# Four turns of the probabilities, moved between the products of a head of queries

## The chip, the cores and the metric

The kernel runs on one core of a Trainium2 chip. The metric is the device time of one execution in microseconds. TensorE (PE) multiplies, VectorE (DVE), ScalarE (ACT) and GpSimd (POOL) do the elementwise work, SyncE (SP) issues most of the transfers. All engines run their own instructions in order and wait for each other on semaphores.

## What is computed

A residual block with four parts over x of 8 sequences x 128 tokens x 512. The change lies in the second, an attention with adapters: 32 query heads in 8 groups of 4, one key and value head for each group, head size 128.

```python
x = x + L0(x)                       # a linear layer chosen by sequence
q = rope(x @ wq + (x @ aq[id]) @ bq[id])      # 32 heads of 128
k = rope(x @ wk + (x @ ak[id]) @ bk[id])      # 8 heads
v = x @ wv + (x @ av[id]) @ bv[id]            # 8 heads
p = softmax(where(causal & mask, q k^T / sqrt(128), min))
o = p v
x = x + o @ wo + (o @ ao[id]) @ bo[id]
x = x + L2(x);  x = x + L3(x)       # two more adapter layers
```

All is float32. Wide products are done in three passes over a high and a low part of both operands (hi x hi, hi x lo, lo x hi), so most operands have an `_hi` tile made on ScalarE and an `_lo` tile made by VectorE or GpSimd.

## The kernel before

A first stage computes L0, keys, values and the first queries. The last computes L2 and L3. Between them stands the loop over heads: `over_heads` (L826) runs `slots(g, first, last)` for the 8 groups g of heads, the first and the last written out, the six between as a loop on each engine. A group has eight slots b = 0 to 7, one for each sequence; slot t = 8g + b treats tile t, the 4 heads of the group for sequence b.

In slot t TensorE does, in this order:

1. `scores` of tile t (L1109): 4 heads, each in two products of 128 columns, into `ps_s`. In the slots b = 0 and b = 4 they need the rotated queries of the next half of sequences, which means all four heads up to the slot just before (`q_done`).
2. `turn` of tile t - 1 (L1118): four transposes of 128 x 128, one a head, of the probabilities into one bank `ps_t`. It waits for `prob_done` and `pt_lo_done`, and the fourth turn signals `t_ready`.
3. `queries` of one head (`project`, L74 to L85): for each of four parts k of the width the products L78, L79, L80 with 512 columns, then two adapter products L83; signals `q_ready`. A head is projected for four sequences at once, so four slots fill one half. The slots t = 60 to 63 have no queries.
4. `outputs` of tile t - 2 (L1140 to L1150), which waits for `ot_lo_done` and for `res_done`.
5. `values` of tile t - 1 (L1126 to L1128), which waits for `pt_lo_done`.

ScalarE in slot t: `pt` (L913, the copy `pt_hi` of `ps_t`, waits for `t_ready`), then the four exponentials of tile t (L929, wait for `max_done`), then parts of weights (wq_hi L896, bq L900; in b = 1 also the four wo_hi L903 and, at the end, ao_hi), and `ot_hi` (L919) of tile t - 1.

VectorE in slot t: maximum and scaling (L1049, `sm`), `ot_lo` of t - 2 (L1026), the additions to `res` and `axo` of t - 3 (L1031, L1032), `pt_lo` of t - 1 (L1022), the reciprocal of tile t (L1064, waits for the exponentials), `rotate` (L1006 `qc`, L1008 twice `qs`, waits for `q_ready`), in odd b `bq_lo` (L1013), in b = 1 `wo_lo` (L1018).

GpSimd in slot t: the probabilities times the reciprocal (L980, `prob_done`), the sum of the rotation `qt` (L973, waits for `qs`, signals `q_done`), wq_lo (L965) in b < 4, and in b = 1 three wo_lo (L989) and ao_lo (L992).

SyncE loads the next group's weights, keys and values. None of its waits names a signal of the turns.

Of the kernel before, what the change touches and what calls it, by code (L numbers as in the profile page):

```python
# [30 lines left out]
def program(nc, x, xt, lora_ids, pos, attn_ids, slot_ids, mask, w0, wq, wk, wv, wo, a3, bq, bk, bv, ao, bo,  # L31
# [9 lines left out]
    B, T, HID = x.shape  # L41
    KC = HID // P
    D = P
    KVH, _, _, GW = wq.shape
    G = GW // D
    R = a3.shape[4]
    NT = B * T
    assert R == R_PACK and KC * R * 2 == P
    HALF = B // 2
    HT = HALF * T  # L50
    PAIRS = B // 2
# [12 lines left out]
    with whole:  # L64
        def sb(ctx, name, shape, dt=F32):
            return ctx.enter_context(nc.sbuf_tensor(name, shape, dt))
# [4 lines left out]
        def sem(ctx, name):  # L71
            return ctx.enter_context(nc.semaphore(name))

        def project(pe, bank, w_hi, w_lo, b_pack, ax, cols, half):  # L74

            tok = slice(half * HT, (half + 1) * HT)
            for k in range(KC):
                pe.matmul(bank[:, :], w_hi[:, k, cols], x1t_hi[:, k, tok], start=(k == 0), stop=False)  # L78
                pe.matmul(bank[:, :], w_hi[:, k, cols], x1t_lo[:, k, tok], start=False, stop=False)  # L79
                pe.matmul(bank[:, :], w_lo[:, k, cols], x1t_hi[:, k, tok], start=False, stop=False)  # L80
            for pair in range(PAIRS // 2):
                n = half * PAIRS // 2 + pair
                last = pe.matmul(bank[:, pair * 2 * T:(pair + 1) * 2 * T], b_pack[:, n, cols],  # L83
                                 ax[:, n * 2 * T:(n + 1) * 2 * T], start=False, stop=(pair == PAIRS // 2 - 1))
            return last  # L85

        res = sb(whole, "res", [P, B, HID])
        ident = sb(whole, "ident", [P, P])
# [26 lines left out]
        axt = [axt_all[:, n, :] for n in range(2)]  # L115
# [56 lines left out]
        ps_t, ps_ao, ps_out, ps_o, ps_q = ps_x1, ps_ax, ps_p[0], ps_p[1], ps_p[2:4]  # L172
# [608 lines left out]
        with ExitStack() as c:  # L781

            wq_raw, bq_raw, wq_hi, wq_lo, bq_pack = raw_w, raw_b, wgt_hi[0], wgt_lo[0], packs[0]
# [10 lines left out]
            prob = [sb(c, f"prob{i}", [P, G, T]) for i in range(2)]  # L794
# [14 lines left out]
            q_ready = sem(c, "q_ready")  # L809
# [5 lines left out]
            prob_done = sem(c, "prob_done")  # L815
            t_ready = sem(c, "t_ready")
            pt_hi_done = sem(c, "pt_hi_done")
            pt_lo_done = sem(c, "pt_lo_done")
# [7 lines left out]
            def over_heads(eng, slots):  # L826

                slots(0, True, False)
                with eng.Fori(1, KVH - 1) as g:
                    slots(g, False, False)  # L830
                slots(KVH - 1, False, True)

            with nc.Block() as block:
# [249 lines left out]
                @block.tensor  # L1083
                def _(pe):
                    project_tensor(pe)

                    def queries(n, half, h, weights=None):

                        if not isinstance(n, int) or n >= 2:
                            pe.wait_ge(q_mult, 3 * (n - 1))  # L1090
                        else:
                            pe.wait_ge(k_mult, 3 * (VU + G - 1 + n))
                        if weights:
                            pe.wait_ge(wq_lo_done, weights[0])
                            pe.wait_ge(bq_lo_done, weights[1])
                        project(pe, ps_q[h % 2], wq_hi, wq_lo, bq_pack, axt[0], slice(h * D, (h + 1) * D), half).then_inc(q_ready, 1)

                    def scores(t, g, b):
                        half = b // HALF
                        if isinstance(t, int) and t == 0:  # L1100
                            pe.wait_ge(k_done, VU + G)
                        if not isinstance(g, int) or g + half >= 1:
                            pe.wait_ge(q_done, B * g + G * half)
                        pe.wait_ge(kt_in[half], 16 * (g + 1))
                        if not isinstance(t, int) or t >= 2:
                            pe.wait_ge(max_done, t - 1)
                        at = (b % HALF) * T
                        for h in range(G):
                            mm = pe.matmul(ps_s[b % 2][:, h, :], qt[:, half, h, at:at + T], kt[:, b * T:(b + 1) * T], start=True, stop=True)  # L1109
                        mm.then_inc(s_ready, 1)  # L1110

                    def turn(t, b):
                        t_parity = b % 2
                        pe.wait_ge(prob_done, t + 1)
                        if not isinstance(t, int) or t >= 1:
                            pe.wait_ge(pt_lo_done, t)
                        for h in range(G):
                            mm = pe.transpose(ps_t[:, h * T:(h + 1) * T], prob[t_parity][:, h, :], ident[:, :])  # L1118
                        mm.then_inc(t_ready, 1)

                    def values(t, g, b):
                        pe.wait_ge(v_in[b // HALF], 32 * (g + 1))
                        pe.wait_ge(pt_lo_done, t + 1)
                        if not isinstance(t, int) or t >= 1:
                            pe.wait_ge(ot_lo_done, t)
                        pe.matmul(ps_o[:, :], v_hi3[:, b, :], pt_hi[:, :], start=True, stop=False)  # L1126
                        pe.matmul(ps_o[:, :], v_hi3[:, b, :], pt_lo[:, :], start=False, stop=False)
                        pe.matmul(ps_o[:, :], v_lo3[:, b, :], pt_hi[:, :], start=False, stop=True).then_inc(o_ready, 1)  # L1128

                    def outputs(t, g, b):  # L1130
                        pe.wait_ge(ot_lo_done, t + 1)
                        if not isinstance(t, int) or t >= 1:
                            pe.wait_ge(res_done, t)
                        for h in range(G):
                            q = slice(h * T, (h + 1) * T)
                            if b == 0 and h == 0:
                                pe.wait_ge(wo_lo_done, g + 1)
                            elif b == 0:
                                pe.wait_ge(wo_lo_pool, (G - 1) * g + h)
                            pe.matmul(ps_out[:, :], ot_hi[:, q], wo_hi[:, h, :], start=(h == 0), stop=False)  # L1140
                            pe.matmul(ps_out[:, :], ot_hi[:, q], wo_lo[:, h, :], start=False, stop=False)  # L1141
                            pe.matmul(ps_out[:, :], ot_lo[:, q], wo_hi[:, h, :], start=False, stop=(h == G - 1))  # L1142
                        if b == 0:
                            pe.wait_ge(ao_lo_done, g + 1)
                        pe.wait_ge(axo_done, t + 1)
                        for h in range(G):
                            q = slice(h * T, (h + 1) * T)
                            w = ao_pack[:, b, h, :, :].rearrange("p a r -> p (a r)")
                            pe.matmul(ps_ao[0:2 * R, 0:T], w, ot_hi[:, q], start=(h == 0), stop=False)
                            mm = pe.matmul(ps_ao[0:2 * R, 0:T], w, ot_lo[:, q], start=False, stop=(h == G - 1))  # L1150
                        mm.then_inc(out_ready, 1)

                    def slots(g, first, last):
                        for b in range(B):
                            t = B * g + b
                            scores(t, g, b)
                            if not first or b >= 1:
                                turn(t - 1, (b - 1) % B)
                            if b < HALF:
                                queries(t, 1, b, None if first else (G * g, PAIRS * g))  # L1160
                            elif not last:
                                queries(t, 0, b - HALF, (G * g + b - HALF + 1, PAIRS * g + 2))
                            if not first or b >= 2:
                                outputs(t - 2, g - 1 if b < 2 else g, (b - 2) % B)
                            if not first or b >= 1:
                                values(t - 1, g - 1 if b < 1 else g, (b - 1) % B)

                    over_heads(pe, slots)
                    end, g = B * KVH, KVH - 1
                    turn(end - 1, B - 1)  # L1170
                    outputs(end - 2, g, B - 2)
                    values(end - 1, g, B - 1)
                    outputs(end - 1, g, B - 1)
# [389 lines left out]
```

## Time and profile before

| | us |
|---|---|
| median of 3 runs | 825.22 |
| lowest and highest | 823.1, 829.45 |
| profiled execution | 820.86 |
| its span, first to last instruction | 819.2 |
| TensorE busy | 752.1 |
| VectorE busy | 543.8 |
| GpSimd busy | 325.6 |
| ScalarE busy | 324.1 |

The span is that of the profiled execution; the time includes what lies around it. Matmuls are pipelined, so that the durations of neighbouring rows overlap: how long a product holds TensorE is read from the starts of successive rows. A weight load (PEld) has a row of its own.

### The profile page before, as it was taken

What the parts mean: (1) busy time and instruction counts of PE and PEld (TensorE: products, weight loads), DVE (VectorE), ACT (ScalarE), POOL (GpSimd) and SP (SyncE); (2) the same over time, 40 slices, a digit from 0 to 9 for tenths busy, and PEclk for the clock granted to TensorE, in tenths of its full rate; (3) what the DMA queues carried; (4) which work ended last, traced back from release to release, by engine and by line L of the source; (5) the groups of instructions that cost most, each with busy time, mean ns of one, the idle gap of its engine ahead of it and who ended that gap; (6) DMA issues with size and microseconds to landing.
All of it is one profiled execution on the core that took longest, in us unless ns stands there. A gap on an engine that the chain in (4) does not pass through costs nothing. (4 is left out here: it accounts for less than half of the span.)

```text
span 819.2 us, 13219 instructions
## 1 busy us (share of the span) xinstructions
PE 752.1 (92%) x4100; PEld 625.0 (76%) x4100; DVE 543.8 (66%) x1362; ACT 324.1 (40%) x902; POOL 325.6 (40%) x280
## 2 busy tenths in 40 slices
PE   2888897985889999999999999999999999998798
PEld 2777785764668888888888888888888888876586
DVE  3645577676576767767677667758676875654983
ACT  3555343011153454354345435336343533542540
POOL 2334351453374273346237236335523723510320
PEclk8798997997899999999999999999999999999899
DMA  8776787264313024013212303301311110720502
GB/s 265 232 282 201 223 259 226 96 220 167 128 65 117 1 74 164 9 64 118 61 45 83 115 0 121 123 0 64 132 47 55 73 38 3 161 20 7 128 25 78
DMA packets 61498, 87.87 MB, mean 107 GB/s; under 512 B 18118, under 2 KB 35686, under 8 KB 57878
## 3 DMA queue, kind: packets, MB, share of 16 engines
q1 hardware_dynamic: 41714, 73.53, 27.8%
q10 hardware_dynamic: 17188, 8.46, 3.5%
q0 software_dynamic: 2560, 5.45, 2.2%
q8 instruction: 17, 0.28, 0.1%
q14 instruction: 19, 0.16, 0.1%
HBM read 72.45 MB, written 19.68 MB: 112 GB/s over the span
## 5 line engine op out<-in xcount | busy, mean ns | idle before, releaser
L980 POOL TENSOR_TENSOR prob<-prob,rinv 128x512 f32<-128x512 f32 x64 | 66.6, 1041 | 215.6 <-DVE rinv L1064 215.6
L919 ACT ACTIVATE ot_hi<-ps_p_o 128x512 fp32r<-128x512 f32 x64 | 38.0, 594 | 214.7 <-PE ps_p_o L1128 214.7
L78 PE MATMUL ps_p_q<-x1t_hi,wgt_hi 128*128 128x512 f32 x280 | 115.9, 414 | 0.8 <-DVE qt L618 0.8
L973 POOL TENSOR_TENSOR qt<-qc,qs 128x512 f32<-128x512 f32 x60 | 83.7, 1395 | 77.8 <-DVE qs L1008 77.8
L929 ACT ACTIVATE prob<-sm,nmax 128x128 f32<-128x128 f32 x256 | 99.8, 392 | 31.2 <-DVE nmax L1049 30.1
L80 PE MATMUL ps_p_q<-x1t_hi,wgt_lo 128*128 128x512 f32 x280 | 110.9, 396 | 0.0
L79 PE MATMUL ps_p_q<-x1t_lo,wgt_hi 128*128 128x512 f32 x280 | 110.8, 396 | 0.0
L1140 PE MATMUL ps_p_out<-wo_hi,ot_hi 128*128 128x512 f32 x256 | 101.9, 398 | 6.6 <-DVE ot_lo L1026 4.7
L1141 PE MATMUL ps_p_out<-wo_lo,ot_hi 128*128 128x512 f32 x256 | 101.4, 396 | 0.0
L1142 PE MATMUL ps_p_out<-wo_hi,ot_lo 128*128 128x512 f32 x256 | 100.8, 394 | 0.0
L1008 DVE TENSOR_TENSOR qs<-ps_p_q,trig 64x512 f32<-64x512 f32 x120 | 82.6, 688 | 3.7
L1049 DVE CUSTOM_DVE_ANT_0 sm<-ps_y_s,maskbias 128x128 f32<-128x128 f32 x256 | 59.0, 286 | 31.4 <-issue 31.0
L1109 PEld LDWEIGHTS ps_y_s<-kt,qt 128*128 128x128 f32 x512 | 67.1, 193 | 12.4 <-POOL qt L682 3.8
L1109 PE MATMUL ps_y_s<-kt,qt 128*128 128x128 f32 x512 | 69.0, 278 | 4.9 <-POOL qt L682 3.6
L80 PEld LDWEIGHTS ps_p_q<-x1t_hi,wgt_lo 128*128 128x128 f32 x280 | 52.8, 189 | 12.4
L1140 PEld LDWEIGHTS ps_p_out<-wo_hi,ot_hi 128*128 128x128 f32 x256 | 48.3, 189 | 17.5 <-DVE ot_lo L1026 6.5
L78 PEld LDWEIGHTS ps_p_q<-x1t_hi,wgt_hi 128*128 128x128 f32 x280 | 53.3, 190 | 10.3 <-DVE qt L618 1.0
L79 PEld LDWEIGHTS ps_p_q<-x1t_lo,wgt_hi 128*128 128x128 f32 x280 | 53.0, 189 | 9.4
L1046 DVE MEMSET gate<- 128x1 f32 x64 | 3.8, 59 | 81.8 <-PE ps_y_s L1109 81.8
L1142 PEld LDWEIGHTS ps_p_out<-wo_hi,ot_lo 128*128 128x128 f32 x256 | 48.0, 187 | 11.5
L1006 DVE TENSOR_TENSOR qc<-ps_p_q,trig 128x512 f32<-128x512 f32 x60 | 41.4, 689 | 21.0 <-PE ps_p_q L83 21.0
L913 ACT ACTIVATE pt_hi<-ps_x_t 128x512 fp32r<-128x512 f32 x64 | 38.1, 596 | 42.8 <-PE ps_x_t L1118 42.6
(227 smaller groups left out, 1693.8 us busy)
## 6 DMA issues: line engine op xcount, KB each, us to landing
raw_w<-in_wq SPq DMA_DIRECT2D x8, 1024.0 KB, 4.9
raw_b<-bq_sel SPq DMA_DIRECT2D x64, 128.0 KB
wo_raw<-in_wo SPq DMA_DIRECT2D x8, 1024.0 KB, 4.9
qt<-in_w SPq DMA_DIRECT2D x5, 1024.0 KB, 9.1
v_hi_d<-v_hi ACTq DMA_DIRECT2D x16, 256.0 KB, 3.7
v_lo_d<-v_lo ACTq DMA_DIRECT2D x16, 256.0 KB, 5.3
kt<-k_rot SPq DMA_DIRECT2D x16, 256.0 KB, 3.7
v_hi<-v_hi_d SPq DMA_DIRECT2D x16, 256.0 KB, 3.9
```

What stands on the lines that cost most here:

```text
L78: pe.matmul(bank[:, :], w_hi[:, k, cols], x1t_hi[:, k, tok], start=(k == 0), stop=False)
L79: pe.matmul(bank[:, :], w_hi[:, k, cols], x1t_lo[:, k, tok], start=False, stop=False)
L80: pe.matmul(bank[:, :], w_lo[:, k, cols], x1t_hi[:, k, tok], start=False, stop=False)
L929: e = act.activation(prob[i][:, h, :], sm[:, h, :], ACT.Exp, bias=nmax[i][:, h:h + 1], scale=-1.0, accum_out=rsum[i][:, h:h + 1])
L973: pool.tensor_tensor(qt[:, half, h, :], qc[:, :], qs[:, :], ALU.add).then_inc(q_done, 1)
L980: pool.tensor_tensor(prob[i][:, :, :], prob[i][:, :, :], rinv[i][:, :].unsqueeze(2).broadcast_to([P, G, T]), ALU.mult).then_inc(prob_done, 1)
L1008: dve.tensor_tensor(qs[to:to + 64, :], ps_q[i][at:at + 64, :], sin_t[to:to + 64, tok], ALU.mult).then_inc(q_mult, 1)
L1049: m = dve.tensor_tensor_reduce(out=sm[:, h, :], in0=ps_s[i][:, h, :], in1=maskbias[:, b, :], scale=-1.0, scalar=3.0e38, op0=ALU.add, op1=A ...
L1109: mm = pe.matmul(ps_s[b % 2][:, h, :], qt[:, half, h, at:at + T], kt[:, b * T:(b + 1) * T], start=True, stop=True)
L1140: pe.matmul(ps_out[:, :], ot_hi[:, q], wo_hi[:, h, :], start=(h == 0), stop=False)
L1141: pe.matmul(ps_out[:, :], ot_hi[:, q], wo_lo[:, h, :], start=False, stop=False)
L1142: pe.matmul(ps_out[:, :], ot_lo[:, q], wo_hi[:, h, :], start=False, stop=(h == G - 1))
```

## The change

`project` gets an argument `between`, a function that it calls behind the first product (L78) of each part k. The turns are cut into `turn_head`, one head each: head 0 does the two waits, head 3 signals. In `slots`, where a slot has queries and a tile to turn, the turns are handed to `queries` as `between`; the slots of the last group with b >= 4 keep `turn` at its old place, as does the end.

```diff
-        def project(pe, bank, w_hi, w_lo, b_pack, ax, cols, half):
+        def project(pe, bank, w_hi, w_lo, b_pack, ax, cols, half, between=None):
             tok = slice(half * HT, (half + 1) * HT)
             for k in range(KC):
                 pe.matmul(bank[:, :], w_hi[:, k, cols], x1t_hi[:, k, tok], start=(k == 0), stop=False)
+                if between:
+                    between(k)
                 pe.matmul(bank[:, :], w_hi[:, k, cols], x1t_lo[:, k, tok], start=False, stop=False)
                 pe.matmul(bank[:, :], w_lo[:, k, cols], x1t_hi[:, k, tok], start=False, stop=False)
...
-                    def queries(n, half, h, weights=None):
+                    def queries(n, half, h, weights=None, between=None):
...
+                    def turn_head(t, b, h):
+                        if h == 0:
+                            pe.wait_ge(prob_done, t + 1)
+                            if not isinstance(t, int) or t >= 1:
+                                pe.wait_ge(pt_lo_done, t)
+                        mm = pe.transpose(ps_t[:, h * T:(h + 1) * T], prob[b % 2][:, h, :], ident[:, :])
+                        if h == G - 1:
+                            mm.then_inc(t_ready, 1)
+
                     def turn(t, b):
-                        t_parity = b % 2
-                        pe.wait_ge(prob_done, t + 1)
-                        if not isinstance(t, int) or t >= 1:
-                            pe.wait_ge(pt_lo_done, t)
                         for h in range(G):
-                            mm = pe.transpose(ps_t[:, h * T:(h + 1) * T], prob[t_parity][:, h, :], ident[:, :])
-                        mm.then_inc(t_ready, 1)
+                            turn_head(t, b, h)
...
                             scores(t, g, b)
-                            if not first or b >= 1:
+
+                            turned = (lambda h, t=t, b=b: turn_head(t - 1, (b - 1) % B, h)) if not first or b >= 1 else None
+                            if b < HALF:
+                                queries(t, 1, b, None if first else (G * g, PAIRS * g), turned)
+                            elif not last:
+                                queries(t, 0, b - HALF, (G * g + b - HALF + 1, PAIRS * g + 2), turned)
+                            else:
                                 turn(t - 1, (b - 1) % B)
-                            if b < HALF:
-                                queries(t, 1, b, None if first else (G * g, PAIRS * g))
-                            elif not last:
-                                queries(t, 0, b - HALF, (G * g + b - HALF + 1, PAIRS * g + 2))
```

## Rows read from the trace of the kernel before

**Rows 1.** The page, busy time, share and instructions of each engine

```profile
PE 752.1 (92%) x4100; PEld 625.0 (76%) x4100; DVE 543.8 (66%) x1362; ACT 324.1 (40%) x902; POOL 325.6 (40%) x280
```

**Rows 2.** TensorE's timeline, slot b = 3: start, us, engine, line, operation, tiles, count

```profile
441.04 1.05 PE L1109 MATMUL ps_y_s<-kt,qt 128*128 128x128 f32 x8
441.93 0.60 PE L1118 MATMUL ps_x_t<-ident,prob 128*128 128x128 f32 x4
442.28 0.48 PE L78 MATMUL ps_p_q<-x1t_hi,wgt_hi 128*128 128x512 f32 x1
442.60 0.40 PE L79 MATMUL ps_p_q<-x1t_lo,wgt_hi 128*128 128x512 f32 x1
...
445.17 0.39 PE L83 MATMUL ps_p_q<-axt_all,pack 128*128 128x256 f32 x2
445.40 0.40 PE L1140 MATMUL ps_p_out<-wo_hi,ot_hi 128*128 128x512 f32 x1
...
449.41 1.05 PE L1109 MATMUL ps_y_s<-kt,qt 128*128 128x128 f32 x8
...
500.31 1.05 PE L1109 MATMUL ps_y_s<-kt,qt 128*128 128x128 f32 x8
```

**Rows 3.** Timeline of the weight loads in the same slot

```profile
442.25 0.19 PEld L78 LDWEIGHTS ps_p_q<-x1t_hi,wgt_hi 128*128 128x128 f32 x1
442.37 0.19 PEld L79 LDWEIGHTS ps_p_q<-x1t_lo,wgt_hi 128*128 128x128 f32 x1
```

**Rows 4.** TensorE's timeline, two adapter products of the same slot

```profile
448.25 0.22 PE L1150 MATMUL ps_ax_ao<-ot_lo,ao_pack 128*32 128x128 f32 x1
448.31 0.22 PE L1149 MATMUL ps_ax_ao<-ot_hi,ao_pack 128*32 128x128 f32 x1
```

**Rows 5.** Timelines of ScalarE and VectorE, slots b = 2 and b = 3

```profile
435.26 0.58 ACT L913 ACTIVATE pt_hi<-ps_x_t 128x512 fp32r<-128x512 f32 x1
435.74 0.40 ACT L929 ACTIVATE prob<-sm,nmax 128x128 f32<-128x128 f32 x1
...
437.19 0.20 ACT L929 ACTIVATION_READ_ACCUMULATOR prob<-sm,nmax 128x1 f32 x1
...
442.56 0.60 ACT L913 ACTIVATE pt_hi<-ps_x_t 128x512 fp32r<-128x512 f32 x1 [0.73 <-PE ps_x_t L1118]
...
437.42 0.18 DVE L1064 RECIPROCAL rinv<-rsum 128x4 f32<-128x4 f32 x1 [0.47 <-ACT prob L929]
437.51 0.68 DVE L1006 TENSOR_TENSOR qc<-ps_p_q,trig 128x512 f32<-128x512 f32 x1
...
445.60 0.69 DVE L1006 TENSOR_TENSOR qc<-ps_p_q,trig 128x512 f32<-128x512 f32 x1 [0.37 <-PE ps_p_q L83]
```

**Rows 6.** GpSimd's timeline, the rotated queries in slots b = 3 and b = 7

```profile
447.82 1.29 POOL L973 TENSOR_TENSOR qt<-qc,qs 128x512 f32<-128x512 f32 x1 [1.46 <-DVE qs L1008]
...
481.34 1.86 POOL L973 TENSOR_TENSOR qt<-qc,qs 128x512 f32<-128x512 f32 x1 [1.46 <-DVE qs L1008]
```

**Rows 7.** TensorE's timeline around a late slot b = 7, and its waits

```profile
474.57 1.05 PE L1109 MATMUL ps_y_s<-kt,qt 128*128 128x128 f32 x8
...
483.43 1.15 PE L1109 MATMUL ps_y_s<-kt,qt 128*128 128x128 f32 x8 [0.31 <-POOL qt L973]
...
PE ps_y_s L1109 <- POOL qt L973: 1.2, 4, 0.3
```

**Rows 8.** VectorE's timeline: a slot's first work, and the end of slots b = 7 and b = 1

```profile
442.23 0.29 DVE L1049 CUSTOM_DVE_ANT_0 sm<-ps_y_s,maskbias 128x128 f32<-128x128 f32 x1
...
443.68 0.68 DVE L1031 TENSOR_TENSOR res<-ps_p_out,res 128x512 f32<-128x512 f32 x1
...
481.30 0.75 DVE L1013 SCALAR_TENSOR_TENSOR pack<-pack,lows,raw_b 128x512 fp32r<-128x512 f32 x1
...
498.64 1.89 DVE L1013 SCALAR_TENSOR_TENSOR pack<-pack,lows,raw_b 128x512 fp32r<-128x512 f32 x1
500.48 1.75 DVE L1018 TENSOR_TENSOR wo_lo<-wo_raw,wo_hi 128x512 fp32r<-128x512 f32 x1
```

More of the change, by code:

```diff
@@ L1095, in queries @@
                             pe.wait_ge(bq_lo_done, weights[1])
-                        project(pe, ps_q[h % 2], wq_hi, wq_lo, bq_pack, axt[0], slice(h * D, (h + 1) * D), half).then_inc(q_ready, 1)
+                        project(pe, ps_q[h % 2], wq_hi, wq_lo, bq_pack, axt[0], slice(h * D, (h + 1) * D), half, between).then_inc(q_ready, 1)
                     def scores(t, g, b):
```

## The prediction

> **What bounds the kernel now.** I read the page first: TensorE is busy 752.1 of 819.2 us [rows 1]. Then TensorE's timeline over one slot of the loop over heads, the slot b = 3 of a middle round [rows 2]. It runs from 441.04 (first product of the scores) to 449.41, so a slot is 8.37 to 8.39 us, and in it TensorE never idles: the scores take 0.89 us until the turns, L78 starts 0.35 us after the first turn, the other products follow each other, and L1140 starts 4.36 us into the slot. Eleven products from L79 (442.60) to L83 (445.17) take 2.57 us, 0.233 us each. There are 64 slots; the turns fall inside queries in 59 of them (t = 1 to 59; t = 0 has no turn, t = 60 to 63 no queries).
>
> A saturated TensorE is half of the answer. The list of waits shows the other half: the scores waited for GpSimd's rotated queries L973 four times [rows 7]. Only the scores of b = 0 and b = 4 wait for a rotation of the slot just before (`q_done`), so the chain that ends in L973 is measured there. I followed it backwards. In the slot b = 3, qt ends at 447.82 + 1.29 = 449.11 and the scores need it at 449.41 less some 0.2. In the slot b = 7 that began at 474.57, qt took 1.86 us, ended at 483.20, and the scores came at 483.43: 8.86 us for that slot in place of 8.39 [rows 6, 7]. So the chain to the next half of the queries has almost no slack, and every delay in it stops TensorE once in four slots: 8 times behind b = 3 and 7 times behind b = 7. By the starts of L1109, five of those seven b = 7 slots are already late, four by 0.47 and one by 0.3 us, 2.2 us in all (one of them stands in [rows 7]).
>
> **The change, TensorE's side.** No instruction is added or removed. The four turns leave the place ahead of L78 and each follows one of the four L78. What does a turn cost in each place? A weight load starts when the product before it starts: L79's load at 442.37 marks the true start of L78, though L78's row begins at 442.28, and L78's load at 442.25 marks the fourth turn [rows 2, 3]. From the first turn (441.93) to 442.37 are 0.44 us for four turns, 0.11 each, and L79 starts 0.23 us after that, the usual spacing. So one turn costs the load that follows it, 0.11 us, because 128 columns stream in less than that. Between L78 and L79 the turn's own load hides under L78, but L79's load starts only with the turn, and L79 can start 0.11 us later. Four turns cost 0.44 us in either place: I take 0 for TensorE's work. The bounds: the pairs L1149 and L1150, 128 columns with a load of only 32, follow each other in 0.06 us [rows 4]. If a turn came down to that, 4 x 0.05 = 0.2 us of a slot would be saved. At the other end a turn that exposed its own load as well would cost 0.22 us, 0.44 us more a slot. I stay at 0.11, because the next load has started with the product before it in every row here.
>
> The Trainium skill, page "TensorE: Matmul & The Clock Gate", section "Back-to-back issue gap", gives a warm gap of about 56 ns for 128 columns, and its section on the array's architecture says that TensorE's queue can pull weight loads ahead of products in flight. By that rule an interleaved turn costs 0.056 us in place of 0.11, an estimate of 0.21 us saved a slot. It is the rule behind the first rival below. The rows of the block of turns, at 0.11 each, side with the same page's section on LDWEIGHTS (128 columns in 107 ns).
>
> **The other side: the last turn comes later.** `t_ready` rises with the fourth turn. It now starts 442.25 - 441.04 = 1.21 us into the slot. With the change L78 truly starts at 0.89, the first turn at 0.89 + 0.233, and the fourth three groups of three products and one turn later: 1.12 + 3 x (0.70 + 0.11) = 3.55 us. That is 2.34 us later. Behind `t_ready` stands ScalarE, in order: pt_hi (L913) first, and only then the four exponentials of the next tile (L929). So the exponentials, though their input is ready, are held until pt_hi. The value products themselves come behind the adapter products of [rows 4], over 7.2 us into the slot, and don't suffer.
>
> How far is it from pt_hi to the rotation? A slot b = 2 shows it, for there pt_hi is late already: pt_hi 435.26, first exponential 435.74, last sum read at 437.39, rinv 437.42, qc 437.51, so 2.25 us from pt_hi to qc [rows 5]. From qc to qt are 447.82 - 445.60 = 2.22 us [rows 5, 6]. pt_hi starts 0.31 us after the fourth turn (442.56 against 442.25). New slot: fourth turn 3.55, pt_hi 3.86, qc 6.11 (now 4.56, held only by the product L83), qt 8.33, end 9.62 us with 1.29 or 10.19 with 1.86, scores 0.23 later: 9.85 or 10.42 in place of 8.38. Nothing hides this, for TensorE works in order and stands at the scores.
>
> **The sum.**
> - Behind b = 3, 8 times, qt at 1.29 us as in these slots now: 8 x 1.47 = 11.8 us.
> - Behind b = 7, 7 times, with qt at 1.86 in five as now: 7 x 1.47 + 5 x 0.57 - 2.2 already there = 10.9 us.
> - After such a stop the eight products of the scores take 1.15 instead of 1.05 us [rows 2, 7]: ten further stops, 1.0 us.
> - The slot b = 2 of rounds 1 to 6. VectorE's bq_lo (L1013) and wo_lo (L1018) stand behind the rotation in b = 1. When they alternate with GpSimd's work they take 1.89 and 1.75 us and end at 502.23, 1.92 us behind the scores of 500.31 (that slot's start). 1.55 us later they end at 3.47; from the first sm to the end of the addition to res are 444.36 - 442.23 = 2.13 us; with some 0.2 for the signal L1140 starts at 5.8 in place of 4.36: 1.45 us of stop [rows 2, 8]. Where bq_lo goes first (0.75 us, qt then 1.86) the same sum ends at some 4.75: 0.4. Three of each: 5.5 us, bounds 2.4 and 8.7.
> - The first round: slot t = 1 has no outputs, so the value products follow the queries 4.36 us into it; pt_hi starts at 3.86 and takes 0.6, pt_lo about as long [rows 5], the signal 0.2: 5.3, so 0.9 us, once.
> - Waits added to TensorE's queue (`prob_done`, `pt_lo_done` behind the first L78): the probabilities are ready long before; 0. No DMA is moved or waits for these signals: 0.
>
> Together 30.1 us. Whether VectorE or GpSimd goes first in each slot moves this: all qt at 1.29 and b = 2 at its low bound give some 24, all at 1.86 with the high bound some 39. The profiled execution took 820.9 us, so it becomes 851.0. The median of the runs shown is 4.4 us above it (825.2), which I carry over: 855.
>
> **The rivals.**
> - *The turns' cost halves on TensorE.* At 0.06 each, 44 slots save 0.2, the 15 slots that end in a stop save only what the fourth turn gains, 3 x 0.05: together 11 us. The late chain remains: 19 us slower, 844. For it: the pairs at 0.06 [rows 4]. Against it: their load is a quarter of a turn's, and the block of turns at 0.11.
> - *Not slower: the hold does not reach TensorE.* If the exponentials were not held by pt_hi, or the queries' rotation had slack of 1.5 us, the late turns would cost nothing: 825 with turns at 0.11, and 813 with turns at 0.06 (59 x 0.2 = 11.8 us less). It is faster by over 1% once a turn costs less than 0.075 us. Against it stand the order on ScalarE and the slots with 8.86 us, where 0.57 us more on qt already stopped TensorE [rows 6, 7].
> - *A turn between products costs more.* At 0.22 us, 44 x 0.44 plus 15 x 0.33 us are 24 more: 879. For it only that no row shows a turn behind a 512-column product; against it L83 to L1140, where the kinds change without a gap.
>
> **How the numbers follow.** The forecast holds 78%, the halved turns 12%, the hold that does not reach 6%, the dearer turns 4%. 24 to 39 us on 820.9, with and without the 4.4 us of the median, is 845 to 864; the first rival brings the lower end to 842, and I stop at 863. About 1% is what a measurement of this kernel can tell from no change. Faster 3%, same 4%, slower 93%.
>
> **What would show it.** Right: the slots inside a half stay at 8.4 us, slots b = 3 and b = 7 show 9.8 to 10.4 with TensorE waiting at L1109 for L973, some 25 us in all; pt_hi starts 3.9 us into a slot, the exponentials directly behind it; L79 follows a turn by 0.11. A stop at L1140 in slots b = 2. Wrong: slots inside a half at 8.2 (turns cheaper) or 8.8 (dearer); exponentials that start before pt_hi; scores of b = 4 on time.

## The result and the profile after

| | before | after |
|---|---|---|
| median | 824.5 us (4 runs) | 853.18 us (4 runs, 849.87 to 858.49) |
| ratio, 95% interval | | 1.0354 (1.0320 to 1.0389) |
| profiled execution | 820.86 us | 858.49 us |
| its loop over heads, first scores to last slot's end | 527.5 us | 559.6 us |

The kernel became 3.5% slower. The profiled execution after is the slowest of the four. It is 37.6 us longer than the profiled execution before. Of these, 32.1 lie in the loop; the unchanged first stage took 4.3 us more (it ends anywhere between 213 and 221 us in the profiles of this study) and the last stage 1.2.

Line numbers moved by the edit: the scores are L1112, the turns L1120, the products L79, L82, L83, the adapter products L86, pt_hi L916, the exponentials L932, qt L976, qc L1009, the outputs L1147. The kernels of the experiments have line numbers of their own.

The list of waits of TensorE after the change (engine, tile, line, who released it: us in total, times, longest) answers [rows 7], where the first line stood at 1.2 us in 4 times:

```profile
PE ps_y_s L1112 <- POOL qt L976: 19.2, 15, 1.8
...
PE ps_p_out L1147 <- DVE ot_lo L1029: 10.6, 8, 2.5
```

Fifteen stops at the scores, exactly the slots behind b = 3 and b = 7, and a second group at the outputs. Here is one slot b = 3 after the change, the same group of heads and slot as in [rows 2], which now begins at 463.44. TensorE's timeline first:

```profile
463.44 1.06 PE L1112 MATMUL ps_y_s<-kt,qt 128*128 128x128 f32 x8
464.25 0.48 PE L79 MATMUL ps_p_q<-x1t_hi,wgt_hi 128*128 128x512 f32 x1
464.57 0.27 PE L1120 MATMUL ps_x_t<-ident,prob 128*128 128x128 f32 x1
464.60 0.48 PE L82 MATMUL ps_p_q<-x1t_lo,wgt_hi 128*128 128x512 f32 x1
464.91 0.39 PE L83 MATMUL ps_p_q<-x1t_hi,wgt_lo 128*128 128x512 f32 x1
...
466.98 0.27 PE L1120 MATMUL ps_x_t<-ident,prob 128*128 128x128 f32 x1
...
473.07 1.16 PE L1112 MATMUL ps_y_s<-kt,qt 128*128 128x128 f32 x8 [1.10 <-POOL qt L976]
```

and its weight loads:

```profile
464.57 0.19 PEld L82 LDWEIGHTS ps_p_q<-x1t_lo,wgt_hi 128*128 128x128 f32 x1
464.68 0.19 PEld L83 LDWEIGHTS ps_p_q<-x1t_hi,wgt_lo 128*128 128x128 f32 x1
464.92 0.19 PEld L79 LDWEIGHTS ps_p_q<-x1t_hi,wgt_hi 128*128 128x128 f32 x1
```

The load of L82 starts with the turn (464.57) and the load of L83, which marks the true start of L82, 0.11 us later; the next is 0.24 on. A turn between products costs 0.11 us, as it did in the block. The fourth turn starts 3.54 us into the slot (466.98), where it was 1.21.

ScalarE, VectorE and GpSimd in the same slot, the rows that answer [rows 5, 6]:

```profile
467.29 0.60 ACT L916 ACTIVATE pt_hi<-ps_x_t 128x512 fp32r<-128x512 f32 x1 [3.06 <-PE ps_x_t L1120]
467.79 0.39 ACT L932 ACTIVATE prob<-sm,nmax 128x128 f32<-128x128 f32 x1
...
469.46 0.18 DVE L1067 RECIPROCAL rinv<-rsum 128x4 f32<-128x4 f32 x1 [0.85 <-ACT prob L932]
469.56 0.68 DVE L1009 TENSOR_TENSOR qc<-ps_p_q,trig 128x512 f32<-128x512 f32 x1
...
471.75 1.26 POOL L976 TENSOR_TENSOR qt<-qc,qs 128x512 f32<-128x512 f32 x1 [0.99 <-DVE qs L1011]
```

Read downwards it is the chain of the prediction: ScalarE idle for 3.06 us until the fourth turn, the exponentials directly behind pt_hi, VectorE idle until they end, the rotation at once behind the reciprocal, GpSimd, and TensorE's stop of 1.10 us. Cut by slots. Each line has start and end, the length, the busy time of TensorE, of its weight loads, of VectorE, ScalarE and GpSimd (with the number of instructions), then TensorE's granted clock, the DMA share and GB/s:

```profile
445.32:453.68 8.36, 8.36 (x50) 6.93 (x49) 5.32 (x18) 3.74 (x12) 3.62 (x4) 1.00 0.44 138
453.68:463.44 9.76, 8.62 (x51) 6.98 (x50) 8.37 (x19) 5.93 (x17) 9.76 (x8) 1.00 0.11 24
463.44:473.07 9.63, 8.53 (x50) 6.75 (x49) 6.58 (x18) 3.85 (x12) 4.47 (x5) 1.00 0.32 128
473.07:481.56 8.49, 8.49 (x49) 7.04 (x50) 5.65 (x18) 2.66 (x10) 2.73 (x3) 1.00 0.44 151
291.67:301.74 10.07, 10.07 (x49) 8.39 (x50) 5.15 (x17) 3.18 (x11) 1.04 (x1) 0.83 0.01 2
```

These are b = 1, 2, 3 and 4 of one group: 8.36 where nothing stops, 9.76 in b = 2, 9.63 in b = 3, and 0.1 us more in the slot behind a stop. The last line is another slot, in which TensorE never idles and yet needs 10.07 us: its clock was granted at 0.83 on average. More of that below.

### The profile page after: what moved, and what is told of

Read it like the earlier page. It is cut to its first block and busy times, and to the rows that moved or that the text cites. A ratio compares the mean times of both kernels' runs of the same rounds, so it can differ in the third digit from the quotient of the medians.

```text
span 856.8 us, 13219 instructions
## 1 busy us (share of the span) xinstructions
PE 760.6 (89%) x4100; PEld 617.6 (72%) x4100; DVE 555.9 (65%) x1362; ACT 318.8 (37%) x902; POOL 322.5 (38%) x280
## 3 DMA queue, kind: packets, MB, share of 16 engines
q10 hardware_dynamic: 17188, 8.46, 3.3%
## 5 line engine op out<-in xcount | busy, mean ns | idle before, releaser
L82 PE MATMUL ps_p_q<-x1t_lo,wgt_hi 128*128 128x512 f32 x280 | 130.7, 467 | 0.0
L79 PE MATMUL ps_p_q<-x1t_hi,wgt_hi 128*128 128x512 f32 x280 | 117.1, 418 | 1.1 <-DVE qt L621 1.1
L1147 PE MATMUL ps_p_out<-wo_hi,ot_hi 128*128 128x512 f32 x256 | 102.9, 402 | 12.5 <-DVE ot_lo L1029 10.6
L83 PE MATMUL ps_p_q<-x1t_hi,wgt_lo 128*128 128x512 f32 x280 | 111.0, 396 | 0.0
L916 ACT ACTIVATE pt_hi<-ps_x_t 128x512 fp32r<-128x512 f32 x64 | 38.4, 599 | 191.8 <-PE ps_x_t L1120 191.8
L932 ACT ACTIVATE prob<-sm,nmax 128x128 f32<-128x128 f32 x256 | 99.1, 391 | 27.5 <-DVE nmax L1052 27.5
L976 POOL TENSOR_TENSOR qt<-qc,qs 128x512 f32<-128x512 f32 x60 | 80.4, 1341 | 54.2 <-DVE qs L1011 54.2
L1112 PEld LDWEIGHTS ps_y_s<-kt,qt 128*128 128x128 f32 x512 | 67.2, 195 | 33.6 <-POOL qt L976 14.9
L1112 PE MATMUL ps_y_s<-kt,qt 128*128 128x128 f32 x512 | 70.8, 282 | 22.7 <-POOL qt L976 19.2
L1025 DVE TENSOR_TENSOR pt_lo<-ps_x_t,pt_hi 128x512 fp32r<-128x512 f32 x64 | 44.1, 688 | 50.9 <-ACT pt_hi L916 50.9
L82 PEld LDWEIGHTS ps_p_q<-x1t_lo,wgt_hi 128*128 128x128 f32 x280 | 53.6, 191 | 21.9 <-issue 0.2
L1120 PE MATMUL ps_x_t<-ident,prob 128*128 128x128 f32 x256 | 67.3, 272 | 0.0
L1147 PEld LDWEIGHTS ps_p_out<-wo_hi,ot_hi 128*128 128x128 f32 x256 | 48.4, 189 | 24.8 <-DVE ot_lo L1029 13.3
L79 PEld LDWEIGHTS ps_p_q<-x1t_hi,wgt_hi 128*128 128x128 f32 x280 | 53.6, 192 | 10.4 <-DVE qt L621 1.3
L83 PEld LDWEIGHTS ps_p_q<-x1t_hi,wgt_lo 128*128 128x128 f32 x280 | 54.1, 193 | 2.2
```

The costliest lines, as they stand in the source:

```text
L932: e = act.activation(prob[i][:, h, :], sm[:, h, :], ACT.Exp, bias=nmax[i][:, h:h + 1], scale=-1.0, accum_out=rsum[i][:, h:h + 1])
L976: pool.tensor_tensor(qt[:, half, h, :], qc[:, :], qs[:, :], ALU.add).then_inc(q_done, 1)
L1120: mm = pe.transpose(ps_t[:, h * T:(h + 1) * T], prob[b % 2][:, h, :], ident[:, :])
```

## The experiments

Theory H is that of the prediction: the fourth turn comes late, ScalarE holds the exponentials behind pt_hi, and the rotated queries come too late for the scores of b = 0 and b = 4. Theory M is its rival: turns between products cost TensorE itself. All ratios are to the kernel before on the same chip; each edit is small and complete, and all kernels compute the whole block.

### Exponentials ahead of pt_hi

On the changed kernel, ScalarE:

```diff
-                            if not first or b >= 1:
-                                pt(t - 1, None if not first else t - 1)
                             act.wait_ge(max_done, t + 1)
...
                             e.then_inc(exp_done, 1)
+                            if not first or b >= 1:
+                                pt(t - 1, None if not first else t - 1)
```

> The changed kernel with ScalarE's pt_hi placed behind the four exponentials of the slot. Theory H (the late fourth turn holds the exponentials, and through them the rotated queries): the exponentials start at 2.16 us of a slot again, pt_hi ends at 4.45, VectorE still does pt_lo ahead of the reciprocal, so qc starts at 5.2 (4.56 before the change, 6.11 with it) and qt ends at 8.7. Scores behind b = 3 and b = 7 come at 8.9 us of the slot, not 9.79: stops of 0.5 us x 15, some 1 to 3 us left in the slots b = 2, in all about 833 us. Theory M (turns between products cost TensorE itself time, by their kind or by the granted clock): nothing but the stops in that chain moves, slots inside a half are unchanged and the kernel stays above 845.

Measured: 834.7 us, ratio 1.015 (1.0103 to 1.0197). The exponentials start 2.16 us into a slot, qc at 5.17, and the slots b = 3 and b = 7 take 8.69 to 8.87 us, or 9.24 to 9.43 where qt takes 1.84. The slots b = 2 of the rounds 1 to 6 take 8.88 us, still 0.5 over 8.37. TensorE's wait at the scores:

```profile
PE ps_y_s L1112 <- POOL qt L976: 8.4, 14, 0.9
```

19.2 us became 8.4 with the turns where they were. That speaks for H; what is left is VectorE, which still does pt_lo ahead of the reciprocal.

### Also pt_lo behind the rotation

```diff
-                            if not first or b >= 1:
-                                pt(t - 1)
                             dve.wait_ge(exp_done, t + 1)
...
                             if not (last and b >= HALF):
                                 rotate(t, (b // HALF + 1) % 2, i)
+                            if not first or b >= 1:
+                                pt(t - 1)
```

> As the run before, and VectorE does pt_lo behind the rotation in place of ahead of the reciprocal. H: qc starts at 4.56 us, held by the product L83 alone, all fifteen stops are gone, the value products get pt_lo just in time (7.3 of 7.6 us). bq_lo then starts behind GpSimd's qt, which takes 1.29 us everywhere, so that the 2.2 us of late b = 7 slots of the kernel before go too. Slots at 8.36 against 8.39: 821 us, between 818 and 825, where the kernel before has 824.5. M: above 835.

Measured: 819.93 us, ratio 0.9962 (0.9940 to 0.9983): faster than the changed kernel by far, and than the kernel before by 0.4%. Every slot of the middle rounds takes 8.35 to 8.42 us, qt takes 1.27 to 1.30 in all of them, and the list of waits has no stop at the scores inside the loop. The turns are in the changed kernel's place, the fourth still 3.5 us into the slot, and the 29 us are gone. ScalarE in a slot b = 3 that begins at 440.78:

```profile
442.84 0.40 ACT L930 ACTIVATE prob<-sm,nmax 128x128 f32<-128x128 f32 x1 [1.27 <-DVE nmax L1052]
...
444.62 0.60 ACT L916 ACTIVATE pt_hi<-ps_x_t 128x512 fp32r<-128x512 f32 x1
```

### The turns earlier, still between products

```diff
                 pe.matmul(bank[:, :], w_hi[:, k, cols], x1t_hi[:, k, tok], start=(k == 0), stop=False)
-                if between:
-                    between(k)
+                if between and k < 2:
+                    between(3 * k)
                 pe.matmul(bank[:, :], w_hi[:, k, cols], x1t_lo[:, k, tok], start=False, stop=False)
+                if between and k == 0:
+                    between(1)
                 pe.matmul(bank[:, :], w_lo[:, k, cols], x1t_hi[:, k, tok], start=False, stop=False)
+                if between and k == 0:
+                    between(2)
```

> The changed kernel with the four turns between products as well, but behind L78, L79 and L80 of the first part k and L78 of the second. The fourth turn starts at 2.15 us of a slot, not 3.55 (1.21 in the kernel before). H: pt_hi at 2.46, qc at 4.71, scores of b = 0 and b = 4 at 8.42 us: 825 us, up to 831 where GpSimd's qt takes 1.86 us. M: the turns stand between products as in the changed kernel, so it is as slow, 850.

Measured: 827.32 us, ratio 1.0038 (1.0014 to 1.0062). pt_hi at 2.47 and qc at 4.73 us came as expected. But slots b = 3 and b = 7 took 8.82 to 9.03 us in thirteen of fifteen, since GpSimd's qt was the long one there:

```profile
485.25 1.85 POOL L980 TENSOR_TENSOR qt<-qc,qs 128x512 f32<-128x512 f32 x1 [0.99 <-DVE qs L1015]
```

VectorE's bq_lo of the same slot was issued at 485.20 and took 0.75 us. The time lies inside the 825 to 831 us that I had written; a later run takes this cause away.

### A block again, but late

The kernel before with its four turns undivided, behind the queries:

```diff
                             scores(t, g, b)
-                            if not first or b >= 1:
-                                turn(t - 1, (b - 1) % B)
                             if b < HALF:
                                 queries(t, 1, b, None if first else (G * g, PAIRS * g))
                             elif not last:
                                 queries(t, 0, b - HALF, (G * g + b - HALF + 1, PAIRS * g + 2))
+                            if not first or b >= 1:
+                                turn(t - 1, (b - 1) % B)
```

> The kernel before with its undivided block of four turns moved behind the queries, so that nothing stands between products and the fourth turn starts at 4.25 us of a slot. H: pt_hi at 4.56, qc at 6.81, qt ends 10.3, scores of b = 0 and b = 4 at 10.5 us: 2.1 us x 15 = 32, ahead of them 1.3 to 2.1 us in six slots b = 2, less the 2.2 us there already, 865 us, slower than the changed kernel. M: a block costs what it cost before, 825.

Measured: 885.13 us, ratio 1.0754 (1.0701 to 1.0806). Without one turn between products it is slower than the changed kernel: the lateness costs, not the mixing. But it is 20 us over the 865 I expected. The chain came as worked out (pt_hi 4.57, qc 6.83), so what is missing lies elsewhere. qt was long in fourteen of fifteen slots, which took 10.88 to 11.08 us where the one with the short qt took 10.33; against 10.5 us for each that is 6.5 us over the sum. The slots b = 2 took 10.5 us, at the long end of what I had written, some 2 us. The rest is TensorE's clock. Two slots that stand behind a stop, in the columns of the slots above:

```profile
555.90:564.40 8.50, 8.50 (x49) 7.20 (x50) 4.60 (x17) 2.66 (x10) 2.21 (x2) 1.00 0.44 157
...
592.62:602.43 9.81, 9.80 (x50) 8.43 (x50) 4.50 (x17) 3.17 (x11) 1.04 (x1) 0.85 0.00 0
```

and the stops ahead of them:

```profile
555.90 1.16 PE L1109 MATMUL ps_y_s<-kt,qt 128*128 128x128 f32 x8 [2.37 <-POOL qt L973]
...
592.62 2.07 PE L1109 MATMUL ps_y_s<-kt,qt 128*128 128x128 f32 x8 [2.55 <-POOL qt L973]
```

Behind the second stop the eight score products take 2.07 us in place of 1.15: the clock fell from 2.4 to 1.2 GHz, and that slot cost 1.3 us more; most such slots took 10.02 to 10.06, 1.6 us more than the 8.46 behind a stop at full clock. It happened in ten slots of the loop, all directly behind such a stop, some 15 us. The three parts make 24 us, of which the execution did not show all: its first stage was 3.7 us shorter than in the profile of the kernel before.

### The turns later, between products

The changed kernel with `between(k)` behind the product of w_lo (the third of its part):

```diff
                 pe.matmul(bank[:, :], w_hi[:, k, cols], x1t_hi[:, k, tok], start=(k == 0), stop=False)
-                if between:
-                    between(k)
                 pe.matmul(bank[:, :], w_hi[:, k, cols], x1t_lo[:, k, tok], start=False, stop=False)
                 pe.matmul(bank[:, :], w_lo[:, k, cols], x1t_hi[:, k, tok], start=False, stop=False)
+                if between:
+                    between(k)
```

> The changed kernel with each turn behind the third product of its part k, not the first: the fourth turn 0.47 us later, at 4.0 us of a slot. H: pt_hi 4.3, qc 6.58, scores of b = 0 and b = 4 at 10.26 us with qt at 1.27 and 10.8 with 1.83, so stops of 1.9 and 2.45 us; 15 x 0.47 + 6 x 0.47 = 10 us more, 863 us, if the granted clock stays. In the late block stops of 2.7 us were always followed by a stretch at 1.2 GHz and those of 2.5 us sometimes, in the changed kernel those of 1.4 never: each such stretch costs some 1.6 us, so up to 15 more where the stops reach 2.45, 870.

Measured: 867.88 us, ratio 1.0536 (1.0497 to 1.0574). Slots b = 3 and b = 7 took 10.08 to 10.27, and 10.64 to 10.84 with the long qt. Five slots behind them in the loop ran in part at 1.2 GHz and took 10.05 to 10.08 us: behind all four slots of 10.64 or more, and behind one of 10.25. Over the kernels with the old order on ScalarE the ratio follows the start of the fourth turn in the slot: 1 at 1.21 us (the kernel before), 1.004 at 2.15, 1.035 at 3.55, 1.054 at 4.0 and 1.075 at 4.26.

### The late block, with the exponentials first

The late block above with ScalarE's and VectorE's two moves of the second experiment.

> The block of turns behind the queries, which took 885 us, with ScalarE's exponentials ahead of pt_hi and VectorE's pt_lo behind the rotation. The fourth turn stays as late (starts at 4.25 us of a slot), but nothing on the chain to the rotated queries waits for it. H: no stops behind b = 3 and b = 7, none in b = 2, and with them no stretch at the lower clock inside the loop: 822 us, within 820 to 827. If the late turns cost in another way, 840 or more.

Measured: 821.33 us, ratio 1.0006 (0.9983 to 1.0029), against 1.0754 without the two moves. From t = 3 on, all slots with queries take 8.37 to 8.40 us and the clock does not fall before the end of the loop. So the whole 7.5%, the low clock included, hung on the hold.

### The block in its old place, with the exponentials first

The two moves alone on the kernel before.

> The kernel before, its block of turns where it was, with only the two moves: ScalarE's exponentials ahead of pt_hi, VectorE's pt_lo behind the rotation. H: the chain to the rotation is free of the turns wherever they stand, so that this differs from the kernel with the same two moves and turns between products only by what the place of the turns is worth on TensorE, 8.39 against 8.36 us in 59 slots: 1.6 us more, 821.5 against 819.9 us. M, or a turn that is cheap between products: 5 us or more between them.

Measured: 822.18 us, ratio 0.9991 (0.9966 to 1.0017). In the profiles its middle slots take 8.39 us (8.40 and 8.44 in two), those with the turns between products 8.36. 59 x 0.03 = 1.8 us, 0.2%, is what the place is worth on TensorE. The intervals of this run and of the second experiment overlap, so only the slots show it. The two moves by themselves gain 2.7 us at the late slots of the kernel before and lose 3.4 at the ends: the first three slots take 24.6 us in place of 22.6, the last four 25.6 in place of 24.3.

### The old order at the end

The second experiment's kernel, with pt_hi and pt_lo at their old places in the four last slots (a condition `last and b >= HALF` at each move).

> The kernel with the exponentials ahead of pt_hi and pt_lo behind the rotation, but in the last four slots, which have no queries, in the old order. There the slots went from 5.70 to 6.14 us in that run; they return to 5.70 and the end comes 1.5 to 2 us earlier: 818.3 us beside 819.9.

Measured: 819.01 us, ratio 0.9947 (0.9925 to 0.9968), the lowest of the study. The last four slots took 24.3 us, not 25.6. The interval overlaps that of the second experiment, so that the gain of 1.3 us is shown by these slots alone.

### bq_lo in the even slots, on the changed kernel

```diff
-                            if not last and b % 2:
+                            if not last and b % 2 == 0:
                                 bq_lo_part(PAIRS * g + b // 2 + 1, b // 2)
```

> The changed kernel with VectorE's bq_lo in the even slots (pair b/2 in b = 0, 2, 4, 6) in place of the odd ones. H: nothing stands beside GpSimd's qt in b = 3 and b = 7, it takes 1.27 us in all of them, and only wo_lo stands behind the rotation of b = 1, so that the stops of 1.37 us at L1140 in six slots b = 2 go: 8.2 us and some 2 us of late qt less, about 843 us. The stops of 1.4 us behind b = 3 and b = 7 stay. If the stops in b = 2 came from the turns themselves, they would stay and the time with them, 851.

Measured: 844.43 us, ratio 1.0252 (1.0205 to 1.0299). qt takes 1.26 us in every b = 3 and b = 7, as expected. The slots b = 2 went from 9.75 to 9.22 us: of a stop of 1.38 us only 0.53 went, in six slots 3.2 of the 8.2 us that I had expected. VectorE is in time now; the stop moved to GpSimd, whose wo_lo and ao_pack stand in b = 1 behind the late qt. In the slot b = 2 from 442.45 on GpSimd is busy throughout; three of its rows:

```profile
443.61 1.75 POOL L968 TENSOR_TENSOR wgt_lo<-raw_w,wgt_hi 128x512 fp32r<-128x512 f32 x1
445.32 3.80 POOL L992 TENSOR_TENSOR wo_lo<-wo_raw,wo_hi 128x512 fp32r<-128x512 f32 x3
449.08 1.28 POOL L995 TENSOR_TENSOR ao_pack<-ao_raw,ao_pack 128x512 fp32r<-128x512 f32 x1
```

and TensorE's rows of it that start on a release, loads and products:

```profile
449.17 0.19 PEld L1147 LDWEIGHTS ps_p_out<-wo_hi,ot_hi 128*128 128x128 f32 x1 [0.55 <-POOL wo_lo L992]
...
450.42 0.25 PE L1156 MATMUL ps_ax_ao<-ot_hi,ao_pack 128*32 128x128 f32 x1 [0.28 <-POOL ao_pack L995]
```

### bq_lo in the even slots, on the kernel before

The same edit.

> The same move of bq_lo in the kernel before. H: the late b = 7 slots of that kernel (2.2 us in five, and 0.1 us each on the slot behind) go, all slots at 8.37 to 8.39: 2.7 us less, 821.5 us.

Measured: 819.96 us, ratio 0.9967 (0.9944 to 0.9990). All seven slots b = 7 take 8.39 us, where four took 8.86 and one 8.68 before.

### bq_lo in the even slots, with the early turns

The same edit on the early turns.

> The turns packed early between products (behind L78, L79, L80 of the first part and L78 of the second), which took 827.3 us beside 824.1, with bq_lo moved to the even slots. In that run GpSimd's qt took 1.85 us in thirteen of the fifteen slots b = 3 and b = 7, where bq_lo went first, and those slots came out at 8.82 and 9.0. H: without bq_lo beside it qt takes 1.29 us, the scores of b = 0 and b = 4 come at 8.43 us of the slot, and the kernel is back at 0.995 to 0.998 of the kernel before. If the early turns cost the time themselves, it stays at 1.004.

Measured: 822.17 us, ratio 0.9961 (0.9940 to 0.9982), from 1.0038. qt in the slots b = 3 and b = 7 took 1.29 us again, the b = 7 slots 8.45. A row of such a slot, beside the one of 1.85 above:

```profile
484.06 1.29 POOL L980 TENSOR_TENSOR qt<-qc,qs 128x512 f32<-128x512 f32 x1 [0.99 <-DVE qs L1015]
```

With bq_lo in the even slots the early turns (0.9961) and the block before (0.9967) are alike. That settles the third experiment: its loss was bq_lo beside qt, not the place of the turns.

## Why the prediction was right, point by point

**The time.** 855 was forecast, 853.18 measured, 29 us over the kernel before in the medians where the sum had 30.1. The mechanism was the one foreseen; that the figure came so close is in part luck. In the profiled loop two terms missed by 2.8 and 2.7 us in opposite directions, and 3.7 us in the slots t = 0, 2 and 8 went with the granted clock, for which nothing had been put down.

**A turn's price, 0 for TensorE.** Right: 0.11 us in either place by the loads. Most slots without a stop on either side went from 8.39 to 8.36 or 8.37 us, a gain of up to 0.03 that I had not seen and whose cause is not shown (0.4 us in all here, more where no stops are, as in the second experiment). The first rival's 0.06 us does not hold: the load of the next 128 weights starts with the turn (464.57) and not ahead of it. The 56 ns of the Trainium skill, page "TensorE: Matmul & The Clock Gate", section "Back-to-back issue gap", on which the prediction drew beside this rival, is there the gap of isolated products; for a stream of loads and products of 128 columns the same section gives about 81 ns. The rows above have 110 ns, start to start of the loads.

**The chain to the rotated queries.** Each step against the slot above: fourth turn 3.54 us (forecast 3.55), pt_hi 3.85 (3.86), qc 6.12 (6.11), qt 8.31 (8.33), next scores 9.62 to 9.80 (9.85). The first and second experiments took the hold away and the stops went; the late block brought them without any turn between products. This is shown.

**The terms of the sum**, from the slot lengths of the profiled loop:

| term | forecast | measured |
|---|---|---|
| behind b = 3, 8 slots | 11.8 | 11.1 |
| behind b = 7, 7 slots | 10.9 | 8.1 |
| scores behind a stop | 1.0 | 0.6 |
| slots b = 2, rounds 1 to 6 | 5.5 | 8.2 |
| first three slots | 0.9 | 3.0 |
| one slot with low clock (t = 8), behind the stop of 10.36 us | 0 | 1.7 |
| all other slots | 0 | -0.6 |
| loop | 30.1 | 32.1 |

*Behind b = 3* and *behind b = 7* the signal from qt to the scores was mis-sized. I had taken 0.23 us for it in both places, from a slot b = 7. Behind b = 7 the scores start 0.23 or 0.24 us after the end of qt in six of seven cases, and a stop there cost 1.41 us. Behind b = 3 they start 0.05 us after it (471.75 + 1.26 = 473.01, scores at 473.07), and a stop cost 1.25. Before the change qt ended 0.32 us ahead of the scores, so the slack behind b = 3 was near 0.3 us and not 0.1. Why the two places differ is not shown.

As for qt, I had let it be long behind b = 7 in five of seven as before; it was in one, and in two of the b = 3 slots, where I had none. Which engine goes first is not inherited from the kernel before, and my two guesses on it erred in opposite directions. The Trainium skill, page "SBUF — State Buffer", section "SBUF: two separate sides", says that VectorE, with two operands in SBUF, and GpSimd share a pair of ports that one instruction holds to its end while the other waits. The rows agree in that one of the two is always drawn out: bq_lo 0.75 with qt 1.86, or 1.88 with 1.28. In either order the pair is through 1.86 to 1.91 us after its start, where 0.75 and 1.28 one after the other would make 2.03.

*The slots b = 2* of rounds 2 to 6 had the longer order: bq_lo and then wo_lo, each drawn out beside GpSimd's work. From the changed kernel's slot that begins at 453.68, VectorE's rows and TensorE's first output product:

```profile
453.58 1.88 DVE L1016 SCALAR_TENSOR_TENSOR pack<-pack,lows,raw_b 128x512 fp32r<-128x512 f32 x1
455.38 1.78 DVE L1021 TENSOR_TENSOR wo_lo<-wo_raw,wo_hi 128x512 fp32r<-128x512 f32 x1
457.10 0.28 DVE L1052 CUSTOM_DVE_ANT_0 sm<-ps_y_s,maskbias 128x128 f32<-128x128 f32 x1
...
458.54 0.67 DVE L1034 TENSOR_TENSOR res<-ps_p_out,res 128x512 f32<-128x512 f32 x1
...
459.32 0.47 PE L1147 MATMUL ps_p_out<-wo_hi,ot_hi 128*128 128x512 f32 x1 [1.14 <-DVE ot_lo L1029]
```

sm starts 3.42 us into the slot (forecast 3.47), and the outputs 5.64 (forecast 5.8), 0.1 us behind the end of the addition to res at 459.21, which is the wait that ended last, though the row names ot_lo. The mechanism and the price of one such stop (1.37 us, forecast 1.45) were right. But I had three slots with it and three at 0.4 us, where bq_lo goes first; it was five and one, and the one cost 1.4 us like the others. What I missed is the second chain beneath: GpSimd's wo_lo and ao_pack are late as well. In the one slot, b = 2 of round 1 from 310.12 on, bq_lo did go first and the outputs start 4.49 us into the slot, only 0.1 late, and then TensorE stands for GpSimd:

```profile
310.00 0.75 DVE L1016 SCALAR_TENSOR_TENSOR pack<-pack,lows,raw_b 128x512 fp32r<-128x512 f32 x1
...
310.05 1.86 POOL L976 TENSOR_TENSOR qt<-qc,qs 128x512 f32<-128x512 f32 x1 [0.99 <-DVE qs L1011]
311.87 1.75 POOL L968 TENSOR_TENSOR wgt_lo<-raw_w,wgt_hi 128x512 fp32r<-128x512 f32 x1
313.58 3.79 POOL L992 TENSOR_TENSOR wo_lo<-wo_raw,wo_hi 128x512 fp32r<-128x512 f32 x3
...
314.61 0.47 PE L1147 MATMUL ps_p_out<-wo_hi,ot_hi 128*128 128x512 f32 x1
...
317.43 0.50 PE L1147 MATMUL ps_p_out<-wo_hi,ot_hi 128*128 128x512 f32 x1 [0.29 <-POOL wo_lo L992]
```

So either order of VectorE and GpSimd cost the same here, and with bq_lo out of the slot altogether 0.85 us remained, as the changed kernel with bq_lo in the even slots showed.

*The first three slots* lost 1.0 us in t = 1, as forecast (0.9). 1.4 of the other 2 lie in t = 0, which has no turn at all: its clock stayed low for longer in that execution (granted 0.56 on average over the slot, 0.72 before). That is not the change, for the late block with the exponentials first shows the same 0.56 there. The last 0.6 lie in t = 2, whose wait of 2.54 us for the first outputs was followed by a low stretch.

**The rivals.** The halved turns, the dearer turns and the hold that does not reach are all excluded by the slots of 8.36 us beside those of 9.6 to 9.8.

**Outside the loop** nothing was forecast. Its instructions are the same, and the first stage's end spreads by 8 us over the profiles, the length of what follows the loop by 1.5 us; the 5.5 us found there are not put down to the change.

## What to carry to other kernels

Before work is spread between other work to fill a saturated engine, look for who waits for its last piece: here the engine's own bill was zero either way, and the fourth transpose, 2.3 us later, stood at the head of another engine's queue, in front of work that needed nothing from it. Where an in-order engine holds a wait that has become late, move the wait behind the ready work (exponentials first): that made the place of the turns indifferent, from 1.0006 to 0.9962 for places that had cost 7.5% and 3.5%. And a slack of 0.1 to 0.3 us in a chain, or a stop that shows in four of sixty slots, is where the length of an edit shows first.

## What the runs showed of the hardware

TensorE's granted clock fell to 1.2 GHz behind idle stretches inside a loop that otherwise kept it busy. Counted are the stops at the scores with a slot with queries behind them. Behind slots that a stop had made 2.3 to 2.7 us longer (10.64 to 11.08 us instead of 8.4, TensorE idle for 2.1 to 2.55 of it in one piece) it fell in fourteen of eighteen cases in the two late kernels; behind those of 9.6 to 9.8 us, a stop of 1.2 to 1.4, in none of eleven in the changed kernel. In between, 10.08 to 10.37 us long, it fell behind two of thirteen. The slots b = 2 of the two late kernels were 1.8 to 2.1 us longer too, by waits at the outputs of at most 1.8 us in one piece, and the clock fell behind none of the twelve. It does not hang on the length of one wait alone: in t = 2 it fell behind 2.54 us in the changed kernel, and did not behind 2.30 us in the kernel before. A low stretch cost the next slot mostly 1.6 us, more than a stop in the changed kernel. The Trainium skill, page "TensorE: Matmul & The Clock Gate", section "What's actually happening", has the same two levels, 1.2 and 2.4 GHz, with idleness as what lowers it. The rows agree: the score products take 2.07 us at the low level against 1.16. What exactly decides between the two outcomes behind a stop of 2.5 us was not tried.

Which of VectorE and GpSimd goes first when both start within 0.1 us changed from slot to slot and from kernel to kernel, and was worth 0.57 us of qt each time. The rows' starts do not tell it: bq_lo starts 0.05 us ahead of qt in all of them, also where it is the one drawn out (1.88 us).
